# Attention in a fused convolution and attention block: values of a head in two rows of five and four units instead of three rows of three, and key scores one place sooner

## What is computed

```python
def _L1_attn_ref(x, Wk, Wq, Wv, Wp, bp):
    B, T, C = x.shape              # 32, 1024, 96
    H = 6; hs = C // H             # 16
    k = (x @ Wk).reshape(B, H, T, hs)
    q = (x @ Wq).reshape(B, H, T, hs)
    v = (x @ Wv).reshape(B, H, T, hs)
    wei = jnp.einsum('bhtd,bhsd->bhts', q, k) * C ** (-0.5)
    wei = jnp.where(jnp.tril(jnp.ones((T, T), dtype=bool)), wei, -jnp.inf)
    wei = jax.nn.softmax(wei, axis=-1)
    out = jnp.einsum('bhts,bhsd->bhtd', wei, v).reshape(B, T, C)
    return out @ Wp + bp
```

## Time and profile before

| | |
|---|---|
| Median of three executions | 2716.24 us (2713.96 to 2720.21) |
| Profiled execution | 2713.15 us |
| Its span, from first to last instruction | 2711.4 us |
| TensorE busy over the span | 2534.1 us (93%) |
| VectorE busy | 2103.7 us (78%) |
| ScalarE busy | 1956.5 us (72%) |
| GpSimd busy | 1509.3 us (56%) |
| VectorE reductions of query scores (L1034) | 1067.4 us busy in 1536 instructions, 103.9 us idle ahead of them |

### The profile page before, as it was taken

The page is one execution under the profiler, slowest core; times in us unless marked ns, Lnnn a source line. Parts: engine busy times, 40 slices in busy tenths (PEclk is TensorE's granted clock), DMA queues, the critical chain, the costliest instruction groups (busy, mean ns, idle before and its releaser), DMA issues. The chain is left out here.

```text
span 2711.4 us, 83212 instructions
## 1 busy us (share of the span) xinstructions
PE 2534.1 (93%) x29309; PEld 1505.9 (56%) x29309; DVE 2103.7 (78%) x3025; ACT 1956.5 (72%) x3751; POOL 1509.3 (56%) x2545
## 2 busy tenths in 40 slices
PE   4899999999999959999999999999999997899996
PEld 2555555555555525666666666666666654455553
DVE  3577676666767448999999999999999975779997
ACT  2687777877777627777777777777777773677775
POOL 0133342333334247888888888888888871225445
PEclk9999999999999969999999999999999998999998
DMA  1122322323222246666666666666666634334546
GB/s 37 30 88 70 95 80 73 101 70 104 70 87 87 82 116 116 120 127 127 121 128 125 123 128 123 127 125 122 127 127 119 128 71 127 97 112 135 147 135 164
DMA packets 777485, 290.84 MB, mean 107 GB/s; under 512 B 702865, under 2 KB 760498, under 8 KB 777394
## 3 DMA queue, kind: packets, MB, share of 16 engines
q1 hardware_dynamic: 776050, 288.43, 46.6%
q10 hardware_dynamic: 1344, 1.18, 0.1%
HBM read 100.77 MB, written 87.29 MB: 69 GB/s over the span
## 5 line engine op out<-in xcount | busy, mean ns | idle before, releaser
L1034 DVE TENSOR_REDUCE at_row_max<-at_ps_queries 128x1 f32<-128x1024 f32 (+7 forms) x1536 | 1067.4, 745 | 103.9 <-PE at_ps_queries L917 103.9
L990 ACT ACTIVATE at_probs<-at_ps_keys 128x512 f32<-128x512 f32 x1344 | 720.8, 596 | 236.8 <-PE at_ps_keys L932 236.5
L907 PE MATMUL at_ps_queries<-at_turned 48*128 48x512 f16 (+3 forms) x2304 | 608.7, 332 | 58.5 <-DVE at_row_max L1034 36.4
L932 PE MATMUL at_ps_keys<-at_turned 50*128 50x128 f16 (+3 forms) x3456 | 574.8, 273 | 6.2 <-ACT at_diag_probs L990 0.5
L952 PE MATMUL at_ps_values<-at_probs,at_v 128*32 128x128 f32 x10752 | 413.8, 278 | 0.5 <-DVE at_out L1026 0.4
L932 PEld LDWEIGHTS at_ps_keys<-at_turned 50*128 50x128 f16 x3456 | 230.1, 94 | 195.0 <-ACT at_probs L990 74.4
L851 POOL TENSOR_TENSOR at_recip<-at_out,at_minus_one 128x8 f32<-128x8 f32 x192 | 313.7, 1634 | 2.8 <-DVE at_out L1026 2.8
L952 PEld LDWEIGHTS at_ps_values<-at_probs,at_v 128*32 128x32 f32 x10752 | 258.7, 109 | 89.9 <-issue 73.3
L513 POOL TENSOR_TENSOR cb_o_hat<-cb_o,cb_o_scale 128x768 f32<-128x768 f32 x32 | 48.0, 1501 | 461.5 <-DVE cb_o_scale L433 461.5
L990 ACT ACTIVATE at_diag_probs<-at_ps_keys 128x512 f32<-128x512 f32 x384 | 230.8, 601 | 35.9 <-PE at_ps_keys L932 27.7
L915 PE MATMUL at_ps_queries<-mask_queries,shifted 64*128 64x256 bf16 (+1 forms) x960 | 241.9, 252 | 0.0
(11 more groups left out here) (223 smaller groups left out, 5078.1 us busy)
## 6 DMA issues: line engine op xcount, KB each, us to landing
qkv_rows<-cb_packed SPq DMA_DIRECT2D x32, 1152.0 KB, 7.6
at_stacks<-qkv_rows SPq DMA_DIRECT2D x192, 192.0 KB, 2.9
cb_x<-in_x_dram SPq DMA_DIRECT2D x32, 384.0 KB, 3.7
cb_x_again<-in_x_dram SPq DMA_DIRECT2D x32, 384.0 KB, 4.5
x_after_conv<-cb_x SPq DMA_DIRECT2D x32, 384.0 KB, 5.0
ff_att_rows<-attention_rows SPq DMA_DIRECT2D x32, 384.0 KB, 4.3
ff_x<-x_after_conv SPq DMA_DIRECT2D x128, 96.0 KB, 2.3
x_after_attention<-ff_x SPq DMA_DIRECT2D x30, 384.0 KB, 2.9
```

The costliest lines, as they stand in the source:

```text
L907: mm = pe.matmul(scores[:, c0:c0 + width], QT[Q_ROWS, slot, qb * P:(qb + 1) * P], KT[Q_ROWS, slot, k0 * P:k1 * P], start=(c0 == 0), stop=True,
L932: mm = pe.matmul(pk[:, bank_k, c0:c0 + n * P], KT[K_ROWS, slot, kb * P:(kb + 1) * P], QT[K_ROWS, slot, q0 * P:(q0 + n) * P], start=(c0 == ...
L990: act.activation(probs, pk[:, ring(r, u + (u > MAX_TURN)), :], ACT.Exp, scale=scale).then_inc(S["probs"], 1)
L1034: ins = dve.tensor_reduce(MX[:, (r - 3) % 2, qb:qb + 1], pq[:, (NR * (r - 1) + g) % QBUFS, b0 * P:(b0 + n) * P], AX.X, ALU.max)
```

## The change

Two constants. The values of a head come in two rows, five units after the key and query scores of `u3` (region 1 complete) and four after those of `u7` (region 3 complete). Before, three units each came after `u1`, `u4` and `u7`; the row at `u4` stood between the two halves of region 2. And with `LAG` 12 each unit of key scores comes one place sooner: `u3` now has unit 0, `u4` unit 1, `u5` unit 2 and so on. What stands in a step is otherwise the same, and so is the number of instructions of each kind in a step.

```diff
     SLOTS = 6
-    VALUE_ROWS = {1: (0, 1, 2), 4: (3, 4, 5), 7: (6, 7, 8)}
+    VALUE_ROWS = {3: (0, 1, 2, 3, 4), 7: (5, 6, 7, 8)}
     VALUES_BACK = 6
     QBUFS, KBANKS = 2, 3
...
     LAST_PART = [1, 3, 5, 7, 8]
-    LAG = 13
+    LAG = 12
     MAX_TURN = 5
```

## The result

The changed kernel takes 2740.36 us, the median of four executions (2734.68 to 2741.04), against 2715.1 us in four of the kernel before (2712.02 to 2720.21). The ratio is 1.0087, its 95% interval 1.0066 to 1.0108. It is slower, as forecast, but by 25 us where I had 9.5, and it lies above the range of 2704 to 2738. The profiled execution took 2741.04 us.

The account below looks back on a forecast made before the run. No engine was full; the longest closed path among three engines set the 6.32 us step. The ScalarE path would make it 6.37: 190 x 0.05 = 9.5 us more, median 2725, range 2704 to 2738.

Parts of the forecast that it names:

- The first path: VectorE's reductions, then TensorE to a complete region 2: 6.23 us a step; as rival, it alone decides, 2699 us, chance 0.13.
- The second: Closed path through ScalarE's exponentials of `u4` and `u5`, then `u7` and region 3: 6.37 us a step, said to decide.
- the wait that vanished ahead of region 1: Sign in the new trace: VectorE should have no wait ahead of region 1, where it had 0.22 us.
- those ahead of regions 2 and 3: Signs in the new trace: VectorE waits about 0.5 us ahead of region 2 and about 0.13 ahead of region 3.
- the row of five: Term for TensorE's five units of values after `u3`: 1.23 us up to the next key scores.
- That is a margin of a hundredth, and I count it as held: `u3`'s key scores after `u0`'s exponential: ready 4.65 us after `u4`, query scores due at 4.66; no cost taken.
- I take nothing: DMA of the row maxima before `u3`: 2.98 us left after the copy, 0.6 spare by a small store's landing; no cost.
- something more late: Rival that a thin cover breaks too: 0.05 us more a step, 2735 us, chance 0.07.
- one of three mishaps: In the 2735 us rival, `u0`'s exponential, region 4 or the DMA of the row maxima comes late, 0.05 us a step.

Follow-up runs that it names:

- transposition at `u7`: Kernel before with the new rows of values, `LAG` 13, and the row maxima transposed at `u7` instead of `u5`: 2698.54 us against 2715.04, ratio 0.9935.
- half exponential at `u4`: Changed kernel with the exponential of the unit at `u4` taken over 256 of its 512 columns: 2712.96 us against 2715.04, ratio 0.9989.
- half exponential at `u0`: Kernel with only the rows of values changed, exponential of the unit at `u0` over 256 of 512 columns: 2724.5 us against 2715.64, ratio 1.0031.
- rows of four and five: Kernel before, key scores unmoved, with values as four units after `u3` and five after `u7`: 2728.45 us against 2715.64, ratio 1.0048.
- Alternating steps at 2806.59 us: Changed kernel (`LAG` 12, rows of five and four) with the row maxima transposed at `u7` instead of `u5`: 2806.59 us against 2714.23, ratio 1.0341.

## Why the prediction was right and wrong

**Right.** The first path: 6.23 forecast, 6.24 measured where it alone decides (transposition at `u7`). The second: 1.57 us from `u4` to `u7` and a step of 6.37 forecast, 1.57 and 6.38 measured. The half exponential at `u4` and the move of the transposition both remove it and bring most steps to the first path. What that base step costs is 9 us by the median of the kernel with the half exponential at `u0` (2724.5 - 2715.64), 10.5 by its trace, against 9.5 forecast. The direction, the wait that vanished ahead of region 1 and those ahead of regions 2 and 3 are as written. So is the row of five: 1.23 forecast, 1.24 measured.

**Wrong.** The time fell outside the range by two terms that were put at nothing. The first is "That is a margin of a hundredth, and I count it as held", for `u3`'s key scores behind `u0`'s exponential. I had looked at it as a margin of the second path. In truth it closes a third path that has no VectorE on it. The prediction's own terms give its length, 4.65 + 0.50 + 1.23 = 6.38, a hundredth over the path that it let decide. By the rows above: 1.51 from `u7` to `u8`, 0.42 to the exponential, 1.09 for two of them, 0.05 to `u3`'s keys, 0.50 to the row of five, 1.24 for it and 1.57 from `u4` to `u7`: 6.38, just the second path's length. It holds both rows of values in full, so their split does not move it, as the rows of four and five show. And ScalarE does not always begin 0.03 after the key scores: in some steps it was 0.11. The step of 6.45 us shows such a delay paid in full. This is worth 6 us (2730.2 with the rows alone, 2724.5 without the wait for `u0`). In a path that is fed by one measured example, the example was a prompt one.

**Wrong too: "I take nothing" for the row maxima.** This was the larger term, 10 us by the medians (2740.4 against 2730.2 with the new rows alone). I gave the DMA 1.4 us, the landing of a small store, and had 0.6 left. In the trace of the changed kernel this DMA itself lands 1.81 us after its issue in the median and 1.72 at least, and the issue comes up to 1.84 after the copy. Together that was 3.00 or more in 16 steps, where the place leaves 2.98. Nor was a stand-in needed: in the trace of the kernel before, the same DMA lands 1.81 after its issue in the median, and 26 of its 192 landings came more than 2.98 after the copy. They did no harm there, where unit 0 stands one place later. The place behind the transposing DMA is not what makes the 1.81: with the DMA moved ahead of it the median is the same, and only the latest landings are gone (1.90 at most, against 3.94). In the kernel with the old rows the key scores of unit 0 come 3.8 us after the copy, so there the earlier place costs nothing by the medians. Alternating steps at 2806.59 us show the same DMA at its worst. I had this as a rival, with 0.07 for "something more late", and priced it at 2735 for one of three mishaps. Two came, and no case held both.

Of those 10 us the traces show 8 between first and last transposition (23.6 less 15.6). 5.1 of them lie in the three steps from 1080 us on (24.27 us, less three of 6.38), and nearly all the rest in the other fifteen over 6.48. The rest of the 10 is not shown to belong to the change; the longer end of the profiled execution, at a lower clock, is in it.

The long steps near the start are of one kind. Eight of the eleven profiles have steps of 7 us and more there, with either place of the key scores and with the DMA moved; those of the kernel before, of the rows alone and of four and five have none. In each of the eight TensorE's key scores sat idle for the DMA of the row maxima, by 0.6 to 2.0 us. In the steps of 8.5 us and more the granted clock was 0.66 to 0.85 in the mean, so a stretch of 1.2 GHz came on top; in six of 6.8 to 7.7 us it stayed at 1.00.

ScalarE's two delays go with the program. From 1120 to 2150 us of the changed kernel there are 160 exponentials that open such a row after a wait for key scores. In 108 the wait is part of the exponential's own instruction, and all of them start 0.04 us after the key scores. In 52 it is an instruction of its own just ahead, and all of these start 0.12 after. No run changes the one into the other, so this is a match and not a test.

**Open.** Why the DMA of the maxima landed only 3.94 us after its issue at 1079.82 is not shown. The core's DMA engines moved 150 GB/s in 1080 to 1084, against 123 in the mean of the stage. Whether the earlier key scores make such a start likelier was not tested either; there is one trace of each kernel.

## What to carry to other kernels

When a change removes the longest closed path among engines, write down every closed path through the shared buffers, not only those through the busiest engine, and add each up with the same care. A path of two engines that runs round once in a step is as binding as one with three, and when two come out equal to a hundredth, a delay on either lengthens the step. Here the ring of three banks was the limit: moving a guest of that ring (the transposition) by two places was worth 32 us beside the new rows, where the rows by themselves had cost 15; with rows of four and five the two together gave 1.8% over the kernel before. And a margin before a DMA should be read from the landings of that DMA itself, and from its latest ones, not from the median of another.

## What was unexpected of the hardware

ScalarE's first exponential after a wait started 0.03 us after the end of the key scores in some steps and 0.11 in others, with the same shapes; the later ones were those whose wait was an instruction of its own. A DMA of 4 KB (the row maxima) landed 1.81 us after its issue in the median, and once 3.94, where stores of 16 KB landed in 1.4. One wait of 1.94 us for it was followed by 5 us and more in which TensorE's granted clock was 0.50 (1.2 GHz), so that a step of 6.4 us took 10.34.
